# Spacing of the indirect row sends in the second half of a mixture-of-experts kernel

## The chip, the cores and the metric

The kernel runs on one core of one Trainium2 chip. The metric is the device time of one execution in microseconds (us). Engines are named as the profile names them: PE (matrix products), PEld (its weight loads), DVE (vector), ACT (scalar), POOL (GpSimd) and SP, which in this kernel only waits and issues DMAs.

## The reference, cut to what matters

```python
# x: (2, 512, 256), 1024 tokens of 256 values, f32
x = x + layernorm(attn(layernorm(x)))        # products, gates, a scan over time
x = x + layernorm(ffn(layernorm(x)))

def ffn(x):                                   # E = 64 experts, inner size 176, top 6 of 64
    probs = softmax(x @ gate_w.T)
    topk_w, topk_idx = top_k(probs, 6);  topk_w /= sum(topk_w)
    combine = sum(one_hot(topk_idx) * topk_w) # (tokens, 64)
    h = silu(einsum('th,eih->tei', x, experts_w1))
    y = einsum('tei,ehi->teh', h, experts_w2)
    routed = einsum('teh,te->th', y, combine)
    shared = (silu(g) * u) @ shared_down.T    # g, u = halves of x @ shared_gate_up.T
    return routed + shared
```

The kernel doesn't compute all experts for all tokens. It sends each token's row to a table, one stretch of 128 rows for an expert, and works through the experts one after the other.

## The kernel before, in words

The 1024 tokens are eight blocks `c` of 128. The first part of the kernel computes the attention-like layer and the gate. For each block it finds the six experts of each token (`choose`) and the row of the table `x_slots` in DRAM that the token's copy number `k` goes to (`place`, which writes `slot_i` and increments `slot_done`). A copy `(k, c)` is one indirect DMA from POOL, the function `send` (its record is line 567): 128 rows of 288 words (`W` = 256 + 32), 144 KB. There are 6 x 8 = 48 of them. The list `FIRST` holds 22, all for blocks 0 to 3, and `SECOND` holds 26, n = 0 to 25. Both lists use three semaphores in turn, by n modulo 3, each send adding 16 when it has landed. Before send n, POOL waits for the landing of send n - 3, so up to three are in flight. Some further waits hold certain sends until another engine's event: in `SECOND` one is at n = 6 (it needs the last slots), and at n = 13, 16 and 20 POOL waits for events of PE: `tx_ps` 1 (the first rows have been transposed), `h_ps` 1 (the first hidden product is done) and `tx_ps` 2. In `FIRST` there is one at n = 15 for `v_ps` 4.

The experts are taken in pairs t = 0 to 32 (64 experts and 2 spare stretches for overfull experts). SP loads the 128 rows of expert s into one of eight places of `early` (`load_rows`, line 392) and, from the seventh expert on, in every third turn a further pair's weights (`load_pair`, line 388). 16 pairs are loaded ahead. Before the rows of an expert, SP calls `rows_sent(e)` (line 403), which waits until enough sends of `SECOND` have landed. How many is fixed by hand in `sends_for`: the function returns 8 for expert 0, 10 for expert 1, 12 for expert 2, 16 for experts 3 to 5, 20 for 6 to 9, and all 26 from expert 10 on. SP works strictly in order: experts 0 to 7 in a first loop, then expert s + 8 after `token_done` for the pair of expert s.

On PE, pair t is `turn_rows(t)` (line 970, four transposes), `main(t)` (line 927), `rest(t)` (line 937) and `output(t)` (lines 949 and 953). For t = 2 to 5 PE runs, in this order, `turn_rows(t + 1)`, `main(t)`, `rest(t)`, `output(t - 1)`. So `main(t)` stands behind the transposes of the next pair. From t = 6 two pairs are taken together. DVE copies the transposed rows (line 1403), writes the token numbers (line 1410) and copies the outputs to `zbuf` (line 1419). ACT applies silu (lines 715, 716). After its sends, POOL scatters each expert's output to `y_rows` (line 609, 66 of them), in program order behind all the sends. At the end SP reads `y_rows` back, and PE and DVE add the six copies of each token with their weights, add the shared part and normalise.

Of the kernel before, what the change touches and what calls it, by code (L numbers as in the profile page):

```python
# [22 lines left out]
def moe_block(nc, x, w_act, w_rec, w_val, gate, pairs, w12, w2b, sgu, sd_a, sd_b, out):  # L23
# [28 lines left out]
    with ExitStack() as ctx:  # L52
# [3 lines left out]
        def sem(name):  # L56
            return ctx.enter_context(nc.semaphore(name))
# [167 lines left out]
        sent_second = [sem(f"sent_second{p}") for p in range(3)]  # L225
# [12 lines left out]
        tx_ps = sem("tx_ps")  # L238
        xT_done = sem("xT_done")
        h_ps = sem("h_ps")  # L240
# [250 lines left out]
        def _(pool):  # L491
# [73 lines left out]
            def send(k, c):  # L565

                return pool.indirect_dma_start(x_slots, bass.IndirectOffsetOnAxis(  # L567
                    ap=slot_i[:, c, k:k + 1], axis=0), rows[:, c, :], None)
# [1 line left out]
            pool.wait_ge(init_done, 16 * (E // 8 + 1))  # L570
            pool.wait_ge(slot_done, 1)
            for n, (k, c) in enumerate(FIRST):
                if n == 15:
                    pool.wait_ge(v_ps, 4)
                elif n == 19:
                    pool.wait_ge(x2T_ps, 4)
                elif n == 21:
                    pool.wait_ge(rank_ps, 2)
                if n >= 3:
                    pool.wait_ge(sent_first[n % 3], 16 * (n // 3))  # L580
                send(k, c).then_inc(sent_first[n % 3], 16)
            pool.wait_ge(slot_done, 2)
            for n, (k, c) in enumerate(SECOND):
                if n == 6:
                    pool.wait_ge(rank_ps, 3)
                    pool.wait_ge(slot_done, 3)
                elif n == 13:
                    pool.wait_ge(tx_ps, 1)
                elif n == 16:
                    pool.wait_ge(h_ps, 1)  # L590
                elif n == 20:
                    pool.wait_ge(tx_ps, 2)
                if n >= 3:
                    pool.wait_ge(sent_second[n % 3], 16 * (n // 3))
                send(k, c).then_inc(sent_second[n % 3], 16)
# [143 lines left out]
        def _(pe):  # L739
# [273 lines left out]
            def add_shared(c):  # L1013

                for j, (_, rows) in enumerate(SC):
                    w = sda_sb[:, j, :] if j < 2 else sdb_sb[:]
                    pe.matmul(in_sum(c), hidT[0:rows, j, P * c:P * c + P], w, start=(j == 0 and c % 2 == 0), stop=False)  # L1017
# [526 lines left out]
```

## Time and profile before

| | |
|---|---|
| median of 3 runs | 288.48 us (287.7 to 293.99) |
| profiled execution, device time | 288.84 us |
| its span (first to last recorded work) | 287.1 us |
| granted PE clock over the span | 0.929 |
| busy share of the span: PE, DVE, POOL, ACT | 82%, 61%, 45%, 28% |

The span is what the profile's times count from; 1.7 us of the execution's own time lies around it. Busy shares are means over stages with different limits: PE is busy for nearly all of the expert stage from 150 us on, but has gaps between 115 and 144 us. The profile's timeline gives, for each record or group of records, start, duration, engine, line, operation, and in brackets the idle time of the engine before it with what ended it.

### The profile page before, as it was taken

The page shows a single profiled execution, that of the slowest core. Times are in us where ns is not written, and L with a number is a line of the kernel's source. Part 1 is how long each engine was busy: PE and PEld are TensorE (multiplying, and loading weights), DVE is VectorE, ACT ScalarE, POOL GpSimd, SP SyncE. Part 2 cuts the span into 40 slices and gives each one's busy share as a digit, 9 for nine tenths or more (in the row PEclk, how much of TensorE's full clock was granted, in tenths as well). Part 3 has the DMA queues.
Part 4 walks back from the last instruction along what each step waited for, and adds up shares of the span by engine and source line. Part 5 has one row for each costly group of instructions (what it writes and reads, how often), then busy time and mean ns, then how long its engine had stood idle before and what let it go on. Part 6 is the DMA issues. An engine that isn't in the chain of part 4 may idle for free.

```text
span 287.1 us, 4229 instructions
## 1 busy us (share of the span) xinstructions
PE 236.2 (82%) x1382; PEld 178.7 (62%) x1382; DVE 176.4 (61%) x552; ACT 81.5 (28%) x188; POOL 129.2 (45%) x162
## 2 busy tenths in 40 slices
PE   6979939975488699065699999999999989989990
PEld 6534818552153568044377788888888767758880
DVE  4539896989997545462157788764443234544884
ACT  2586631394022114400011142112222402120033
POOL 7008300004677354757757606556556565561000
PEclk9999988999599689855979999999999999999997
DMA  6999999998232112345579999999969842668913
GB/s 211 356 376 370 371 360 416 423 415 331 87 123 103 62 62 84 126 142 168 194 203 308 350 371 348 309 384 348 308 238 364 281 153 75 219 222 277 345 39 110
DMA packets 34616, 72.00 MB, mean 251 GB/s; under 512 B 4577, under 2 KB 24609, under 8 KB 34081
## 3 DMA queue, kind: packets, MB, share of 16 engines
q1 hardware_dynamic: 29024, 55.68, 56.0%
q0 software_dynamic: 5568, 16.03, 14.9%
q8 instruction: 12, 0.20, 0.3%
q14 instruction: 12, 0.09, 0.1%
HBM read 44.89 MB, written 26.80 MB: 250 GB/s over the span
## 4 chain that ended last, share of the span: by engine, by line
PE 55%; DVE 20%; issue 9%; another core or an unknown queue 5%; DMA 4%; ACT 4%; POOL 1%; ACTq 0%; SPq 0%; POOLq 0%; DVEq 0%
PE bank L927 9%; PE bank L953 9%; PE bank L937 6%; PE bank L949 5%; PE bank L766 4%; PE bank L970 4%; PE bank L1017 4%; DMA early<-x_slots 3%; PE bank L775 3%; PE bank L802 3%; DVE stats L1082 2%; PE bank L836 2%; PE bank L1021 2%; DVE hidT L1131 2%
## 5 line engine op out<-in xcount | busy, mean ns | idle before, releaser
L609 POOL DMA_INDIRECT y_rows<-zbuf,token_i x66 | 64.9, 983 | 49.4 <-DVE zbuf L1419 33.8
L567 POOL DMA_INDIRECT x_slots<-rows,slot_i x48 | 47.4, 987 | 62.4 <-DVE slot_i L1234 34.5
L1419 DVE COPY zbuf<-bank 128x256 f32<-128x256 f32 x66 | 24.9, 420 | 56.1 <-PE bank L953 49.1
L715 ACT ACTIVATE sgu_sb<-bank 128x256 f32<-128x256 f32 x33 | 12.6, 383 | 108.1 <-PE bank L937 58.2
L927 PE MATMUL bank<-work,w_all 128*128 128x128 f32 x256 | 35.5, 290 | 5.6 <-issue 3.8
L927 PEld LDWEIGHTS bank<-work,w_all 128*128 128x128 f32 x256 | 33.1, 204 | 6.9 <-issue 6.7
L953 PE MATMUL bank<-w_all,sgu_sb 128*128 128x256 f32 x128 | 33.7, 397 | 0.0
L802 PE MATMUL bank<-x2nT,sgu_sb 128*128 128x256 f32 (+3 forms) x72 | 25.7, 511 | 7.4 <-DVE nt L1352 7.4
L970 PE MATMUL bank<-ident,early 128*128 128x128 f32 x128 | 20.0, 287 | 11.0 <-DMA early<-x_slots 11.0
L1403 DVE COPY work<-bank 128x512 f32<-128x512 f32 x33 | 22.5, 685 | 10.6 <-PE bank L970 5.4
L953 PEld LDWEIGHTS bank<-w_all,sgu_sb 128*128 128x128 f32 x128 | 22.5, 189 | 9.8 <-issue 7.6
L970 PEld LDWEIGHTS bank<-ident,early 128*128 128x128 f32 x128 | 15.5, 146 | 15.0 <-issue 6.9
L802 PEld LDWEIGHTS bank<-x2nT,sgu_sb 128*128 128x128 f32 (+1 forms) x72 | 14.4, 210 | 15.4 <-issue 13.6
L937 PE MATMUL bank<-work,w_all 128*64 128x128 f32 (+1 forms) x256 | 20.6, 294 | 0.8 <-issue 0.8
L949 PE MATMUL bank<-w_all,left 48*128 48x256 f32 x128 | 20.5, 421 | 0.7 <-ACT left L716 0.7
L937 PEld LDWEIGHTS bank<-work,w_all 128*64 128x64 f32 (+1 forms) x256 | 14.6, 136 | 3.8 <-issue 1.5
L766 PE MATMUL bank<-early,attw 128*128 128x512 f32 x32 | 14.5, 601 | 2.7 <-ACT early L680 2.0
L618 ACT ACTIVATE rs<-ve 128x2 f32<-128x2 f32 (+1 forms) x12 | 2.4, 204 | 46.5 <-DVE ve L1091 43.0
L775 PE MATMUL bank<-attw,early 128*128 128x256 f32 x64 | 14.1, 379 | 0.0
L949 PEld LDWEIGHTS bank<-w_all,left 48*128 48x128 f32 x128 | 10.7, 189 | 5.4 <-issue 3.7
L784 PE MATMUL bank<-wval_sb,zbuf 128*128 128x256 f32 x32 | 8.9, 440 | 5.6 <-issue 5.6
L775 PEld LDWEIGHTS bank<-attw,early 128*128 128x128 f32 x64 | 12.2, 190 | 2.1 <-issue 0.5
(218 smaller groups left out, 356.1 us busy)
## 6 DMA issues: line engine op xcount, KB each, us to landing
w_all<-pairs SPq DMA_DIRECT2D x32, 752.0 KB, 8.3
x_slots<-hidT SPq DMA_DIRECT2D x8, 1152.0 KB, 13.0
early<-x_slots SPq DMA_DIRECT2D x64, 144.0 KB
w_all<-y_rows SPq DMA_DIRECT2D x4, 1024.0 KB, 6.1
w_all<-y_rows SPq DMA_DIRECT2D x4, 512.0 KB, 10.4
y_rows<-zbuf,token_i POOLq DMA_INDIRECT x66
x_sb<-x SPq DMA_DIRECT2D x4, 256.0 KB, 3.6
out<-work SPq DMA_DIRECT2D x4, 256.0 KB, 2.1
```

The lines of the kernel that those rows point to most:

```text
L567: return pool.indirect_dma_start(x_slots, bass.IndirectOffsetOnAxis(ap=slot_i[:, c, k:k + 1], axis=0), rows[:, c, :], None)
L609: pool.indirect_dma_start(y_rows, bass.IndirectOffsetOnAxis(ap=token_i[:, s % 32:s % 32 + 1].bitcast(U32), axis=0), yS[:, s % 8, :], None) ...
L766: mm = pe.matmul(bank[4 + 2 * b + m][:], wact_sb[:, KC * late + k, m, :], xnT[:, k, b, late:late + T], start=(k == 0 and late == 0), stop= ...
L775: mm = pe.matmul(bank[c // 2][:, C * (c % 2):C * (c % 2) + C], xnT[:, k % KC, b, at:at + P], wrec_sb[:, k, :], start=(k == 0), stop=(k == ...
L802: mm = pe.matmul(product_in(n, g), sgu_sb[:, k, IS * g + at:IS * g + at + rows], x2nT[:, k, t0:t0 + width], start=(k == 0), stop=(k == KC ...
L927: pe.matmul(h_b[t % 2][:, P * i:P * i + P], w[:, PK * k + P * i:PK * k + P * i + P], xT[:, t % 4, i, k, :], start=(k == 0), stop=(k == KC ...
L937: mm = pe.matmul(h_b[t % 2][r:r + n, 2 * P:3 * P], w[:, at:at + n], xT[:, t % 4, i, k, :], start=(k == 0), stop=(k == KC - 1))
L949: pe.matmul(y_b[2 * (t % 2) + i][:, 0:C], hT_r[r:r + IR, t % 4, :], weights(2 * t)[r:r + IR, PW2 + 2 * C:PW], start=True, stop=False)
L953: mm = pe.matmul(y_b[2 * (t % 2) + i][:, 0:C], hT[:, t % 4, P * i:P * i + P], weights(2 * t)[:, PW2 + C * i:PW2 + C * i + C], start=False, ...
L970: mm = pe.transpose(x_b[t % 2][:, at:at + P], src[:, P * k:P * k + P], ident[:])
L1403: dve.tensor_copy(xT[:, t % 4].rearrange("p i k t -> p (i k t)"), x_b[t % 2][:]).then_inc(xT_done, 1)
L1419: dve.tensor_copy(yS[:, s % 8, :], y_b[s % 4][:, 0:C]).then_inc(y_done, 1)
```

## The change

Three waits for events of PE in `SECOND` (at n = 13, 16 and 20) are removed. In their place every send from n = 13 on first waits until the send ahead of it, n - 1, has landed. The wait for send n - 3 stays. In `FIRST` the wait for `v_ps` 4 stands one send earlier. What each send carries, their order, and the counts that SP waits for are as before.

```diff
             for n, (k, c) in enumerate(FIRST):
-                if n == 15:
+                if n == 14:
                     pool.wait_ge(v_ps, 4)
...
                 if n == 6:
                     pool.wait_ge(rank_ps, 3)
                     pool.wait_ge(slot_done, 3)
-                elif n == 13:
-                    pool.wait_ge(tx_ps, 1)
-                elif n == 16:
-                    pool.wait_ge(h_ps, 1)
-                elif n == 20:
-                    pool.wait_ge(tx_ps, 2)
+                if n >= 13:
+                    pool.wait_ge(sent_second[(n - 1) % 3], 16 * ((n - 1) // 3 + 1))
                 if n >= 3:
                     pool.wait_ge(sent_second[n % 3], 16 * (n // 3))
                 send(k, c).then_inc(sent_second[n % 3], 16)
```

## Rows read from the trace of the kernel before

**Rows 1.** The page: the span, the chain by engine, the scatters' group.

```profile
span 287.1 us, 4229 instructions
...
PE 55%; DVE 20%; issue 9%; another core or an unknown queue 5%; DMA 4%; ACT 4%; POOL 1%; ACTq 0%; SPq 0%; POOLq 0%; DVEq 0%
...
L609 POOL DMA_INDIRECT y_rows<-zbuf,token_i x66 | 64.9, 983 | 49.4 <-DVE zbuf L1419 33.8
```

**Rows 2.** Timeline of POOL: sends n = 9, 11, 12, 13, 15, 16, 19, 25.

```profile
118.20 0.96 POOL L567 DMA_INDIRECT x_slots<-rows,slot_i  x1 [0.30 <-issue]
...
120.73 0.96 POOL L567 DMA_INDIRECT x_slots<-rows,slot_i  x1 [0.30 <-issue]
121.99 0.96 POOL L567 DMA_INDIRECT x_slots<-rows,slot_i  x1 [0.30 <-DMA x_slots<-rows,slot_i]
124.09 0.96 POOL L567 DMA_INDIRECT x_slots<-rows,slot_i  x1 [1.15 <-PE bank L970]
...
126.67 0.96 POOL L567 DMA_INDIRECT x_slots<-rows,slot_i  x1 [0.30 <-DMA x_slots<-rows,slot_i]
128.88 0.96 POOL L567 DMA_INDIRECT x_slots<-rows,slot_i  x1 [1.25 <-PE bank L937]
...
132.67 0.96 POOL L567 DMA_INDIRECT x_slots<-rows,slot_i  x1 [0.30 <-issue]
...
140.51 0.96 POOL L567 DMA_INDIRECT x_slots<-rows,slot_i  x1 [0.30 <-issue]
```

**Rows 3.** Timeline of SP: row loads of experts 1, 2, 3, 6 and 10.

```profile
120.92 0.33 SPq L392 DMA_DIRECT2D early<-x_slots  x1
...
123.53 0.33 SPq L392 DMA_DIRECT2D early<-x_slots  x1
...
129.16 0.80 SPq L392 DMA_DIRECT2D early<-x_slots  x2
...
135.21 0.82 SPq L392 DMA_DIRECT2D early<-x_slots  x2
...
143.14 0.85 SPq L392 DMA_DIRECT2D early<-x_slots  x2
```

**Rows 4.** Timeline of PE: transposes of expert 3, and of pair 5.

```profile
131.27 0.69 PE L970 MATMUL bank<-ident,early 128*128 128x128 f32 x2 [2.87 <-DMA early<-x_slots]
...
150.74 0.60 PE L970 MATMUL bank<-ident,early 128*128 128x128 f32 x4
```

**Rows 5.** Timeline of DVE and ACT at the two events that POOL waited for.

```profile
123.85 0.69 DVE L1403 COPY work<-bank 128x512 f32<-128x512 f32 x1 [5.39 <-PE bank L970]
...
128.64 0.38 ACT L715 ACTIVATE sgu_sb<-bank 128x256 f32<-128x256 f32 x1 [10.56 <-PE bank L937]
```

**Rows 6.** DMA packets from 126.5 to 129.1 us, 40 slices of 0.065 us, busy tenths.

```profile
DMA  0000006999762000000000000099496920000000
```

**Rows 7.** Timeline of PE at pairs 2 and 3; then a window, PEclk third last.

```profile
143.89 2.05 PE L927 MATMUL bank<-work,w_all 128*128 128x128 f32 x8 [3.18 <-issue]
...
146.92 0.82 PE L970 MATMUL bank<-ident,early 128*128 128x128 f32 x4
147.57 1.06 PE L927 MATMUL bank<-work,w_all 128*128 128x128 f32 x8
...
149.14 0.70 PE L949 MATMUL bank<-w_all,left 48*128 48x256 f32 x4
...
143.00:150.00 7.00, 6.11 (x41) 4.96 (x42) 4.22 (x8) 0.98 (x4) 3.67 (x6) 0.76 0.68 200
```

**Rows 8.** Window 185 to 226 us: busy time (PE, PEld, DVE, ACT, POOL), PEclk, DMA share, GB/s.

```profile
185.00:226.00 41.00, 41.00 (x344) 35.35 (x343) 19.79 (x55) 11.13 (x43) 23.37 (x25) 1.00 0.93 324
```

**Rows 9.** Timeline of POOL: the last scatter.

```profile
258.13 0.96 POOL L609 DMA_INDIRECT y_rows<-zbuf,token_i  x1 [0.30 <-issue]
```

**Rows 10.** Timelines of PE and POOL at the moved wait of the first half.

```profile
81.95 3.72 PE L784 MATMUL bank<-wval_sb,zbuf 128*128 128x256 f32 x16 [0.77 <-issue]
...
86.64 0.96 POOL L567 DMA_INDIRECT x_slots<-rows,slot_i  x1 [0.30 <-DMA x_slots<-rows,slot_i]
```

## The prediction

> **What bounds the kernel now.** I read the page first, then the timeline of POOL over the sends of the second half, then that of SP for what the sends release, and last that of PE for when it needs what SP loads. The page's chain gives PE 55% of the span and POOL 1% [rows 1]. So POOL's 48 sends look free. They are not far from the path, though: SP may load the rows of expert 10 and of all later ones only when all 26 sends have landed, and in PE's program order everything from `main(4)` on stands behind the transposes of experts 10 and 11, that is `turn_rows(5)`. From there the expert stage is a train of PE work: from 185 to 226 us PE is busy 41.00 of 41.00 us, with DMA at 0.93 of its engines [rows 8]. A delay ahead of a train with no gap arrives at the end whole. The question is therefore how much later the last send lands, and how much slack stands between that and `turn_rows(5)`.
>
> **The slack.** Send 25 starts at 140.51 [rows 2]; SP issues the rows of expert 10 at 143.14 and those of expert 11 0.52 later, since the two issues together take 0.85 and one takes 0.33 [rows 3]. Expert 3's rows, issued at 129.16 [rows 3], were in PE's hands at 131.27 [rows 4], 2.11 us. So experts 10 and 11 are usable at 143.14 + 0.52 + 2.11 = 145.8, and PE comes to them at 150.74 [rows 4]. The slack is 5.0 us.
>
> **The spacing before.** Where nothing holds it, POOL starts a send 1.26 us after the last (120.73 to 121.99): 0.96 of its own work and 0.30 between two. From 121.99 (n = 12) to 140.51 (n = 25) there are 13 steps, 18.52 us [rows 2]. Of that 13 x 1.26 = 16.4 is bare pace and about 2.1 the held sends: 1.15 - 0.30 = 0.85 at n = 13 and 1.25 - 0.30 = 0.95 at n = 16 [rows 2], and about 0.3 in the rest. Removing the three waits gives back these 2.1 us at most.
>
> **The spacing after.** Each of the 13 steps becomes: start of a send, its landing, POOL waking, next start. No row shows a send waiting for the one right ahead, so I take it from two pieces. The first is start of a send to SP's issue that waited for it: n = 9 to expert 1, 118.20 to 120.92 = 2.72; n = 11 to expert 2, 2.80; n = 15 to expert 3, 2.49; n = 19 to expert 6, 2.54; n = 25 to expert 10, 2.63 [rows 2, 3]. The long ones are from an unbroken series of sends and the short ones from sends with a pause near them, as all will have after the change. I take 2.55. The second is POOL's wake: at `tx_ps` 1 DVE starts at 123.85 and POOL at 124.09, at `h_ps` 1 ACT at 128.64 and POOL at 128.88 [rows 2, 5], so POOL is 0.24 behind an engine woken by the same event. A step is 2.55 + 0.24 = 2.79, say 2.8. The packets bear it out: the burst of n = 15 (start 126.67) lies in slices 26 to 32 of the window, until about 128.6 [rows 6], 1.9 us after the start, before its completion can be seen.
>
> The bounds of a step: not under 1.9 + 0.24 = 2.14, since the packets end no earlier. From above 2.80 + 0.24 = 3.04 by the longest of the five, and with contention up to 3.8, since n = 12 started 3.79 after n = 9 without being held beyond the usual 0.30 [rows 2]. I take 2.8, nearest to the two short pairs.
>
> **The skill beside it.** The wait added here serialises the completion part of each transfer, and a rule speaks against that. By the Trainium skill, page "DMA: Bandwidth & Descriptors", section "Anatomy of one DMA — SWDGE (gpsimd) path", one DMA costs about 2.0 us plus its bytes over 436 GB/s, mostly the receipt of the write. For 147 KB this gives, as an estimate from that page, 2.34 us. If it counts from POOL's start the step would be 2.6 and the time about 300; if it comes on top of POOL's own 0.96 us the step would be 3.5, which is the second rival below. The 2.49 to 2.80 of the trace lie nearer to the first reading.
>
> **The sum.** Send 25 starts at 121.99 + 13 x 2.8 = 158.4 in place of 140.5. SP issues expert 10 at 158.4 + 2.55 = 160.9 (before: 143.14) and expert 11 at 161.5; PE gets them at 163.6. Against 150.74 that is 12.9 us late: 17.8 of delay, less the slack of 5.0.
>
> Earlier gates slip too, but behind this one. Send 15 lands at 121.99 + 3 x 2.8 + 2.55 = 132.9, so expert 3 is 3.8 late (129.16 before). Send 19 lands at 144.1 against 135.21, 8.9 late, and lets SP load experts 6 to 9; PE then reaches the end of pair 3 near 155 and stands idle for some 9 us. These slips cost nothing of their own.
>
> The idle PE has a price. After the gap at 143.89 pair 2 runs at the low clock: `main` and `rest` take 146.92 - 143.89 = 3.03 us, where those of pair 3 take 149.14 - 147.57 = 1.57, and the window 143 to 150 shows a granted clock of 0.76 [rows 7]. That 1.5 us is hidden in the new gap now, but `main(4)` and `rest(4)` pay the same after it: 1.5 us.
>
> Behind the waiting sends on POOL stand the scatters. They start 17.8 us later too, at about 159.7. The first scatters' buffers are wanted when pair 4 hands over its outputs, after 163.6 and several microseconds of products. A scatter takes 0.98 + 0.30 = 1.28 us [rows 1], two of them 2.6, while PE needs 3.3 us for a pair (41.00 us hold a bit over 12 pairs, judged by 344 / 28 products and transposes [rows 8]). So POOL catches up; its last scatter, at 258.13 before [rows 9], goes with the train. I add nothing. What SP holds back meanwhile are the loads of weights beyond the first 16 pairs. They are issued in step with the experts, many pairs ahead of use, and shift as a whole with PE. Nothing.
>
> The wait in the first half: `v_ps` 4 comes when the products of line 784 end, 81.95 + 3.72 = 85.67; send 14 of `FIRST` starts at 86.64, after the event [rows 10]. Nothing.
>
> Together 12.9 + 1.5 = 14.4 us. The profiled execution took 288.84 us (span 287.1 and 1.7 around it); it stands 0.4 above the median of 288.48. 288.84 + 14.4 = 303.2, which I give as 303.
>
> **The rivals.**
>
> *The slack swallows it (not slower).* The steps are so short that the last landing still falls inside the slack. Place: expert 11 at `turn_rows(5)`. It decides when the delay is under 5.0 us, so 13 steps under 18.52 + 5.0 = 23.5, a step under 1.81. Then the time is about 288.5; and if a landing were reported so early that POOL's own 1.26 ruled, the sends would end 2.1 us sooner and the time would be 287 to 288, since that too goes into slack. For it: the packets' burst is short, 0.5 us. Against it: packets still run 1.9 us after the start [rows 6]. 0.04.
>
> *Landings are slower than SP's issues let see.* The step is 3.5, between the 3.04 and the 3.8 that POOL's three-back waits allow [rows 2]. Then send 25 starts at 167.5, expert 11 is usable at 167.5 + 3.3 + 0.5 + 2.1 = 173.4, which is 22.7 late; with the clock's 1.5 the time is 313. Against it: n = 25 was seen landed by SP after 2.63. For it: row loads and sends would share the DMA. 0.12. (The second reading of the Trainium skill's page above is this case.)
>
> *A lone send lands faster.* With nothing else in flight the step is 2.2: send 25 at 150.6, expert 11 usable at 150.6 + 2.0 + 0.5 + 2.1 = 155.2, 4.5 late, with 1.5 the time is 295. For it: the shorter pairs are those with pauses. 0.12.
>
> **How the numbers follow.** The forecast (step 2.5 to 3.05) gets 0.72. At 2.5: 121.99 + 32.5 + 2.4 + 2.6 = 159.5, 8.8 late, with the clock 299; at 3.04: 121.99 + 39.5 + 2.8 + 2.6 = 166.9, 16.2 late, 306.5. I widen to 297 and 309 for half the clock's price, and for gaps later in the train that may take up or add a few us. That leaves 2 in 10 outside. A measurement of this kernel tells about 2% (5.8 us) from no change. Faster by more has 0.01, within 0.04, slower 0.95.
>
> **What would show it.** In the timeline of POOL, sends 13 to 25 start 2.8 us apart, and each idle time of about 1.8 us ends with the DMA of the sends. SP issues expert 10 at about 161. PE is idle for some 9 us before the transposes of pair 5 at about 163.6, and afterwards the distances between pairs are as before. Wrong would be: steps under 1.9 or over 3.1; a PE that doesn't wait at pair 5; or a train that runs closer together than before and wins the delay back.

## The result and the profile after

The changed kernel takes 303.14 us (median of 4 runs, 300.08 to 304.84), the kernel before 288.09 us in the same session. The ratio is 1.049, 95% interval 1.041 to 1.057. It compares the fast runs alone and comes to about 14 us, while the medians take in the slow runs too and differ by 15. The profiled execution of the changed kernel took 304.79 us with a span of 303.1, so it lies at the upper end of the runs; distances inside it are what is read here, not its total.

The page of the changed kernel, its span and its chain by engine, which answer to [rows 1]:

```profile
span 303.1 us, 4239 instructions
...
PE 54%; DVE 15%; issue 13%; POOL 6%; ACT 4%; another core or an unknown queue 3%; DMA 3%; ACTq 0%; SPq 0%; POOLq 0%; DVEq 0%
PE bank L949 9%; PE bank L923 9%; POOL x_slots L567 6%; PE bank L933 5%; PE bank L945 5%; PE bank L762 5%; PE bank L966 4%; PE bank L1013 4%; PE bank L780 3%; PE bank L798 3%; PE bank L771 3%; DVE stats L1078 3%; PE bank L1017 2%; PE bank L789 2%
```

POOL has gone from 1% of the chain to 6%, all of it the sends of line 567, and "issue" from 9% to 13%. Four source lines are gone, so PE's `turn_rows` is now line 966, `main` 923, `rest` 933, and `output` 945 and 949.

The timeline of POOL in the changed kernel: sends 12 to 15, 17, 21, and 25 with the first scatter. It answers to [rows 2].

```profile
120.63 0.96 POOL L567 DMA_INDIRECT x_slots<-rows,slot_i  x1 [0.30 <-DMA x_slots<-rows,slot_i]
123.32 1.07 POOL L567 DMA_INDIRECT x_slots<-rows,slot_i  x1 [1.74 <-DMA x_slots<-rows,slot_i]
126.19 0.96 POOL L567 DMA_INDIRECT x_slots<-rows,slot_i  x1 [1.79 <-DMA x_slots<-rows,slot_i]
128.88 0.96 POOL L567 DMA_INDIRECT x_slots<-rows,slot_i  x1 [1.74 <-DMA x_slots<-rows,slot_i]
...
135.22 0.96 POOL L567 DMA_INDIRECT x_slots<-rows,slot_i  x1 [2.64 <-DMA x_slots<-rows,slot_i]
...
146.92 0.96 POOL L567 DMA_INDIRECT x_slots<-rows,slot_i  x1 [2.56 <-DMA x_slots<-rows,slot_i]
...
157.80 0.96 POOL L567 DMA_INDIRECT x_slots<-rows,slot_i  x1 [1.75 <-DMA x_slots<-rows,slot_i]
159.07 0.96 POOL L605 DMA_INDIRECT y_rows<-zbuf,token_i  x1 [0.30 <-issue]
```

Each idle time before a send has become 1.73 to 1.80 us and ends with the landing of a send. Two are longer, 2.64 and 2.56: they are the first sends under way while SP loads rows (experts 3 to 5 and 6 to 9). From send 12 to send 25 there are now 37.17 us in place of 18.52.

SP's issue of expert 10's rows, and PE around its wait for them (answers to [rows 3, 4, 7]):

```profile
160.42 0.33 SPq L392 DMA_DIRECT2D early<-x_slots  x1
```

```profile
151.79 1.13 PE L949 MATMUL bank<-w_all,sgu_sb 128*128 128x256 f32 x4
162.74 0.66 PE L966 MATMUL bank<-ident,early 128*128 128x128 f32 x2 [9.81 <-DMA early<-x_slots]
163.89 0.69 PE L966 MATMUL bank<-ident,early 128*128 128x128 f32 x2 [0.49 <-DMA early<-x_slots]
164.37 1.92 PE L923 MATMUL bank<-work,w_all 128*128 128x128 f32 x8
...
171.14 1.81 PE L923 MATMUL bank<-work,w_all 128*128 128x128 f32 x8
```

PE stands idle for 9.81 us before the transposes of expert 10. Then `main(4)` to `main(5)`, 164.37 to 171.14, takes 6.77 us. The windows of the changed kernel show why, and that the later train is as it was in [rows 8] (columns: stretch, its length, busy PE, PEld, DVE, ACT, POOL, granted PE clock, DMA share, GB/s):

```profile
164.00:168.00 4.00, 4.00 (x22) 3.21 (x22) 2.04 (x4) 0.61 (x3) 3.11 (x5) 0.50 0.94 317
168.00:172.00 4.00, 4.00 (x17) 3.12 (x14) 1.37 (x4) 0.24 (x1) 2.02 (x3) 0.50 1.02 360
172.00:176.00 4.00, 4.00 (x29) 2.94 (x28) 1.63 (x7) 0.86 (x3) 1.51 (x2) 0.91 1.00 337
...
201.00:242.00 41.00, 41.00 (x343) 35.35 (x343) 19.81 (x55) 11.67 (x45) 23.34 (x25) 1.00 0.92 321
```

For 8 us after the gap the granted clock is the lower of the two levels (0.50, 1.2 GHz), and then it rises to 1.00 (2.4 GHz).

The front of the kernel, before send 12, differs between executions by more than some of the effects looked for: send 12 starts at 121.99 us in the profile of before and between 117.0 and 120.7 in all but one of the others. So I count times from the start of send 12. "Late" is against before.

| kernel | send 25, late | `main(4)`, late | `main` of pairs 24 and 25, late |
|---|---|---|---|
| before (from send 12: 18.52, 29.19, 97.97) | 0 | 0 | 0 |
| changed | 18.7 | 14.6 | 17.3 |
| landing waits from n = 18 | 14.1 | 10.0 | 11.3 |
| landing waits from n = 22 | 6.7 | 2.0 | 4.7 |
| two sends in flight (first, second time) | 1.0, 1.2 | -0.7, 2.2 | 0.2, 2.4 |
| no waits at all | -2.0 | 6.6 | 6.6 |

### The profile page after: what moved, and what is told of

The parts are those of the page before. It is cut to its first block, busy times and chain, and to the rows that moved or that the text cites. A ratio compares the mean times of both kernels' runs of the same rounds, so it can differ in the third digit from the quotient of the medians.

```text
span 303.1 us, 4239 instructions
## 1 busy us (share of the span) xinstructions
PE 241.6 (80%) x1382; PEld 181.2 (60%) x1382; DVE 175.2 (58%) x552; ACT 81.4 (27%) x188; POOL 128.7 (42%) x162
## 4 chain that ended last, share of the span: by engine, by line
PE 54%; DVE 15%; issue 13%; POOL 6%; ACT 4%; another core or an unknown queue 3%; DMA 3%; ACTq 0%; SPq 0%; POOLq 0%; DVEq 0%
PE bank L949 9%; PE bank L923 9%; POOL x_slots L567 6%; PE bank L933 5%; PE bank L945 5%; PE bank L762 5%; PE bank L966 4%; PE bank L1013 4%; PE bank L780 3%; PE bank L798 3%; PE bank L771 3%; DVE stats L1078 3%; PE bank L1017 2%; PE bank L789 2%
## 5 line engine op out<-in xcount | busy, mean ns | idle before, releaser
L605 POOL DMA_INDIRECT y_rows<-zbuf,token_i x66 | 64.2, 973 | 48.8 <-DVE zbuf L1415 34.2
L711 ACT ACTIVATE sgu_sb<-bank 128x256 f32<-128x256 f32 x33 | 12.7, 384 | 125.3 <-PE bank L933 54.3
L966 PE MATMUL bank<-ident,early 128*128 128x128 f32 x128 | 21.2, 299 | 27.8 <-DMA early<-x_slots 27.8
L923 PE MATMUL bank<-work,w_all 128*128 128x128 f32 x256 | 36.9, 299 | 2.9 <-DVE work L1399 1.8
L923 PEld LDWEIGHTS bank<-work,w_all 128*128 128x128 f32 x256 | 34.7, 214 | 4.2 <-issue 4.1
L949 PE MATMUL bank<-w_all,sgu_sb 128*128 128x256 f32 x128 | 34.6, 405 | 0.0
L798 PEld LDWEIGHTS bank<-x2nT,sgu_sb 128*128 128x128 f32 (+1 forms) x72 | 14.4, 209 | 15.9 <-issue 14.1
L762 PE MATMUL bank<-early,attw 128*128 128x512 f32 x32 | 16.2, 659 | 2.7 <-ACT early L676 2.0
L771 PE MATMUL bank<-attw,early 128*128 128x256 f32 x64 | 14.1, 379 | 0.0
L762 PEld LDWEIGHTS bank<-early,attw 128*128 128x128 f32 x32 | 6.4, 207 | 11.3 <-issue 7.9
```

Of the source, the lines that this page charges most:

```text
L605: pool.indirect_dma_start(y_rows, bass.IndirectOffsetOnAxis(ap=token_i[:, s % 32:s % 32 + 1].bitcast(U32), axis=0), yS[:, s % 8, :], None) ...
L762: mm = pe.matmul(bank[4 + 2 * b + m][:], wact_sb[:, KC * late + k, m, :], xnT[:, k, b, late:late + T], start=(k == 0 and late == 0), stop= ...
L771: mm = pe.matmul(bank[c // 2][:, C * (c % 2):C * (c % 2) + C], xnT[:, k % KC, b, at:at + P], wrec_sb[:, k, :], start=(k == 0), stop=(k == ...
L798: mm = pe.matmul(product_in(n, g), sgu_sb[:, k, IS * g + at:IS * g + at + rows], x2nT[:, k, t0:t0 + width], start=(k == 0), stop=(k == KC ...
L923: pe.matmul(h_b[t % 2][:, P * i:P * i + P], w[:, PK * k + P * i:PK * k + P * i + P], xT[:, t % 4, i, k, :], start=(k == 0), stop=(k == KC ...
L949: mm = pe.matmul(y_b[2 * (t % 2) + i][:, 0:C], hT[:, t % 4, P * i:P * i + P], weights(2 * t)[:, PW2 + C * i:PW2 + C * i + C], start=False, ...
```

## Experiment 1: the waits removed, nothing put in

```diff
-                elif n == 13:
-                    pool.wait_ge(tx_ps, 1)
-                elif n == 16:
-                    pool.wait_ge(h_ps, 1)
-                elif n == 20:
-                    pool.wait_ge(tx_ps, 2)
```

> The kernel before with its three waits for PE events (n = 13, 16, 20) taken out and nothing put in. My theory: these waits cost 2.1 us of POOL's time, the last send starts 2.1 us sooner, and the gain falls into the slack in front of pair 5, so the time stays within 1% of before, at most 1 us better. A rival, that the three waits protected something else (POOL's sends disturbing PE's first pairs) and their loss is part of the 15 us: 2 us or more slower than before.

Measured: 294.45 us, ratio to before 1.012 (1.002 to 1.022). The sends do end 2.0 us sooner, and the kernel is slower all the same, by about 3.5 us. The interval goes from 0.6 to 6.5 us, so the time alone rules out my gain but not a loss of under 1%; the trace, where everything from `main(4)` on is 6.6 us late, speaks for the rival. Its timeline, where the end of DVE's chain of small operations (`find_extra`), ACT's first silu and the second pair are read; PE's `rest(0)` ends at 126.4 in it ("remote" stands where the profile finds no releaser on this core):

```profile
128.41 0.96 POOL L567 DMA_INDIRECT x_slots<-rows,slot_i  x1 [0.30 <-issue]
128.82 0.23 DVE L1300 TENSOR_SCALAR ext_s<-ext_s,row_no 128x2 f32<-128x2 f32 x1 [0.36 <-DVE ext_s L1299]
...
130.94 0.96 POOL L567 DMA_INDIRECT x_slots<-rows,slot_i  x1 [0.31 <-issue]
130.95 0.15 DVE L1303 TENSOR_SCALAR ext_i<-rare_no 128x1 int32<-128x1 f32 x1 [1.26 <-issue]
132.21 0.96 POOL L567 DMA_INDIRECT x_slots<-rows,slot_i  x1 [0.30 <-issue]
132.35 0.15 DVE L1304 COPY nt<-ext_s 128x1 f32<-128x1 f32 x1 [1.25 <-DVE ext_i L1303]
...
137.25 0.96 POOL L567 DMA_INDIRECT x_slots<-rows,slot_i  x1 [0.30 <-issue]
138.67 0.38 ACT L709 ACTIVATE sgu_sb<-bank 128x256 f32<-128x256 f32 x1 [21.97 <-remote]
...
141.57 0.69 DVE L1397 COPY work<-bank 128x512 f32<-128x512 f32 x1 [9.06 <-remote]
...
142.41 2.04 PE L921 MATMUL bank<-work,w_all 128*128 128x128 f32 x8 [12.46 <-DVE work L1397]
```

The same two small DVE operations follow each other directly in before:

```profile
130.14 0.15 DVE L1309 TENSOR_SCALAR ext_i<-rare_no 128x1 int32<-128x1 f32 x1
130.33 0.15 DVE L1310 COPY nt<-ext_s 128x1 f32<-128x1 f32 x1
```

DVE waits there for its own last operation only. Where before they start 0.19 us apart, they now start 1.40 apart, each within 0.15 us after a start of a POOL send. ACT gets PE's first hidden product at 138.67, more than 12 us after it was done and 0.46 us after POOL's last send ends (137.25 + 0.96 = 138.21). The transposes of pair 1 end by 129.95, and DVE takes them at 141.57. All this lies in an unbroken series of 20 sends, 1.26 us apart. The waits of before cut this series into pieces of 7, 3, 4 and 6, with two scatters behind the last. In this execution no packet runs on the queues of instruction loads between 127 and 142 us, so instruction loads aren't what held ACT and DVE.

The kernel before has a smaller case of this itself, behind its last pause. PE ends the transposes of pair 2 at 138.58, and DVE takes them at 143.10, when POOL has started the last of eight DMAs in a row:

```profile
137.98 0.60 PE L970 MATMUL bank<-ident,early 128*128 128x128 f32 x4
...
143.10 0.69 DVE L1403 COPY work<-bank 128x512 f32<-128x512 f32 x1 [2.08 <-remote]
```

That bears on the slack that I read. With landing waits in the second half of the series (changed kernel, n = 18, n = 22) DVE takes pair 2 at once, and in the run from n = 22 PE is ready for the transposes of pair 5 at 25.7 us after send 12 in place of 28.8. A part of before's slack is time in which PE itself was held up.

## Experiments 2 and 3: fewer landing waits

```diff
                 elif n == 20:
                     pool.wait_ge(tx_ps, 2)
+                if n >= 22:      # in the other kernel: n >= 18
+                    pool.wait_ge(sent_second[(n - 1) % 3], 16 * ((n - 1) // 3 + 1))
```

> The kernel before, its three waits kept, with the wait for the send ahead only from n = 22 (4 sends). My theory: 4 x (2.75 - 1.26) = 6.0 us later for the last send, 5.0 of them slack before the transposes of pair 5, so about 1 us slower (0 to 2). Rival, that each wait costs its share at the end whole, with no slack (15 us over 13 waits): 4.6 us slower.

Measured: 292.12 us, ratio 1.011 (1.006 to 1.016), some 3.1 us slower, between the two expectations, so the total doesn't decide. The trace does: send 25 is 6.7 late (6.0 expected) and `main(4)` only 2.0, so 4.7 us were slack. But PE waited for expert 10's rows, and that had its own price:

```profile
149.88 1.30 PE L972 MATMUL bank<-ident,early 128*128 128x128 f32 x4 [4.42 <-DMA early<-x_slots]
...
150.98 1.92 PE L929 MATMUL bank<-work,w_all 128*128 128x128 f32 x8
...
157.75 1.65 PE L929 MATMUL bank<-work,w_all 128*128 128x128 f32 x8
```

```profile
150.00:157.00 7.00, 7.00 (x29) 4.97 (x30) 2.04 (x4) 0.85 (x3) 5.79 (x7) 0.50 0.93 279
```

`main(4)` to `main(5)` takes 6.77 us here too, and the granted clock is 0.50 from 150 to 157. A gap of 4.4 us cost as much clock as one of 9.8. At pair 24 this execution is 4.7 us late, which is the rival's figure; but it is made of 2.0 at `main(4)` and 3.2 of clock, less 0.5 made good on the way, and not of a share for each wait.

> The kernel before, its three waits kept, with the wait for the send ahead from n = 18 (8 sends). My theory: 8 x 1.49 = 11.9 us later, 0.8 more for one send that meets row loads, less 5.0 of slack = 7.7 us at pair 5, and 1.5 to 3 us at the low clock after the gap: 9 to 11 us slower than before. Rival, costs in proportion to the waits: 8 x 15 / 13 = 9.2 us; the two are told apart by the run from n = 22 and by the trace, where mine wants the PE gap before pair 5 to be about 4 us shorter than with all 13 waits.

Measured: 299.81 us, ratio 1.030 (1.020 to 1.040), 8.7 us slower by the ratio and 9.7 by the medians (9 to 11 expected). Send 25 is 14.1 late, `main(4)` 10.0. With the changed kernel these are three points: 6.7 to 2.0, 14.1 to 10.0 and 18.7 to 14.6, so the slack is 4.7, 4.2 and 4.1 us, and past it `main(4)` follows the last send nearly one to one. A cost in proportion to the number of waits, with no slack, would have put `main(4)` 6.7 late behind the first four waits.

The clock's part is not a fixed sum, though. Behind landing waits from n = 18 the gap before pair 5 is 12.1 us, and not about 4 shorter than in the changed kernel as I expected, since PE came to it sooner; and behind it `main(4)` to `main(5)` takes only 4.99 us. The granted clock is 0.50 at 160 to 162 us and back at 1.00 from 163 on, after 4 to 5 us of work:

```profile
158.14 0.66 PE L972 MATMUL bank<-ident,early 128*128 128x128 f32 x2 [12.09 <-DMA early<-x_slots]
...
159.78 1.92 PE L929 MATMUL bank<-work,w_all 128*128 128x128 f32 x8
...
164.77 1.06 PE L929 MATMUL bank<-work,w_all 128*128 128x128 f32 x8
```

So this restart cost 1.4 us where the other two cost 3.2.

## Experiments 4 and 5: the gate moved, and POOL's scatters held back

One number of the changed kernel: from which expert on SP asks for all 26 sends.

```diff
-        WITHOUT = (10, 6)
+        WITHOUT = (16, 6)
```

> The changed kernel with one number changed: SP waits for all 26 sends only from expert 16 on instead of expert 10 (experts 10 to 15 after 20 sends). POOL's sends and scatters stand exactly as in the changed kernel. My theory, that the late loads of experts 10 and 11 set the time: PE goes through pairs 5 to 7 without the 10 us gap, and then meets the next in line: rows of expert 16 (about 3.5 us late) and POOL's scatters, which start 17 us late and free the output buffers 4 to 6 us late. So 5 to 6 us slower than before, about 294 us, 8 us or more faster than the changed kernel. Rival, that the scatters queued behind the spaced sends are what costs: no gain, about 303 us.

Measured: 307.97 us, ratio 1.060 (1.049 to 1.071). My expectation of 294 missed by 14 us. Its first half held: pairs 4 and 5 ran with no gap (`main(5)` at 153.6 us). Then two things stood in line. First, `main(6)` stands behind the transposes of experts 16 to 19, whose rows SP may load only after the last send: PE's last wait before it is for the rows of expert 19. Second, ACT and DVE again got PE's work late, at the end of a series of POOL's DMAs. Beside these, DVE may write an output buffer only when the scatter of eight experts ago has landed, and the scatters start only behind the last send:

```profile
162.28 0.42 DVE L1415 COPY zbuf<-bank 128x256 f32<-128x256 f32 x1 [6.64 <-DMA y_rows<-zbuf,token_i]
...
169.09 0.69 PE L966 MATMUL bank<-ident,early 128*128 128x128 f32 x2 [2.87 <-DMA early<-x_slots]
169.57 3.39 PE L923 MATMUL bank<-work,w_all 128*128 128x128 f32 x16
...
177.06 0.96 POOL L605 DMA_INDIRECT y_rows<-zbuf,token_i  x1 [0.30 <-issue]
179.98 0.38 ACT L711 ACTIVATE sgu_sb<-bank 128x256 f32<-128x256 f32 x1 [23.89 <-remote]
180.19 0.69 DVE L1399 COPY work<-bank 128x512 f32<-128x512 f32 x1 [5.88 <-remote]
...
180.68 3.75 PE L923 MATMUL bank<-work,w_all 128*128 128x128 f32 x16 [5.67 <-ACT left L712]
```

Counted from send 12, pair 6 is 11.6 us late, pair 8 is 18.4 and pair 10 is 21.0. The 11.6 at pair 6 are the moved gate once more: the last send is itself 3.1 us later than in the changed kernel, with steps of 3.86 and 4.88 us beside the loads that now run early, and the rows of expert 19, issued at about 163, landed 6 us later beside weight loads. I had put the rows of expert 16 only 3.5 us late. The scatters held DVE, which took the rows of pair 7 at 164.79 for that reason, but that was over before expert 19's rows came; what the scatters alone cost this run doesn't show. From pair 6 to 8 the late events add another 7 us: PE waits 5.67 us for ACT. The run doesn't speak against the gate of the changed kernel, where PE's wait of 9.81 us ends with the rows; but it can't be taken as a clean proof of it either.

The next kernel adds waits to POOL, which can only delay it:

```diff
+                if s in (6, 8, 10):
+                    pool.wait_ge(scat[(s - 1) % 8], scattered(s - 1))
                 pool.wait_ge(y_done, s + 1)
```

> The kernel that asks for all 26 sends from expert 16 on, with three added waits on POOL: scatters s = 6, 8 and 10 wait for the landing of the scatter ahead. This only delays POOL, by about 5 us. Theory A (an unbroken series of POOL's DMAs holds back the events of the other engines): ACT gets the hidden product of pair 6 at once and not 6 us after its end, and the kernel is faster than without the waits, 300 to 304 against 308 us. Theory B (the scatters are simply late): 2 to 5 us slower than 308.

Measured: 313.42 us, ratio 1.088 (1.080 to 1.095): slower, as theory B said, and by more than its 2 to 5 us (5.4 by the medians; by the ratios, taken to the kernel before as it ran beside each, it is more). But the place that theory A spoke of did change. ACT takes pair 6 as soon as `rest` gives it, and pairs 6 and 8 stand 5.2 us apart in place of 11.1:

```profile
170.97 3.36 PE L925 MATMUL bank<-work,w_all 128*128 128x128 f32 x16
174.26 1.09 PE L935 MATMUL bank<-work,w_all 128*64 128x128 f32 x16
...
176.21 1.95 PE L925 MATMUL bank<-work,w_all 128*128 128x128 f32 x16
```

```profile
174.97 0.38 ACT L713 ACTIVATE sgu_sb<-bank 128x256 f32<-128x256 f32 x1 [17.86 <-PE bank L935]
```

At pair 8 this kernel is 12.7 us late where the one without the pauses is 18.4. It loses more later, since the three added waits last 4.18, 6.57 and 4.56 us where I had counted about 5 for all three: with the DMA engines busy a landing takes far longer. So each theory got one part: the pauses cleared the events, and their length cost more than that.

## Experiments 6 to 8: the price of the clock

> The changed kernel once more, as the base for the run with the filled gap on the same chip: 300 to 305 us, PE idle about 10 us before the transposes of pair 5, then about 8 us at the low clock.

Measured: 302.98 us, ratio 1.037 (1.025 to 1.048) with a before of 292.85 us in that session. That is 10 to 11 us in place of 14 to 15: the changed kernel took the same time as in the first session, and the kernel before took 4.8 us more. The intervals of the two ratios overlap. `main(4)` to `main(5)` is 6.8 us again.

```diff
             for t in range(2, QUADS[0]):
+                if t == 4:
+                    pe.wait_ge(y_done, 6)
+                    keep_warm(y_b[0], 18)     # in the second kernel: 10
                 turn_rows(t + 1)
```

> The changed kernel, with 18 spare products of 128x512 (about 8 us) on PE into a free bank between pair 3's output and the transposes of pair 5, where PE stands idle. Nothing else waits for them. Theory: of the 15 us, 3.2 are pairs 4 and 5 at the low clock after the gap (6.77 us from one main to the next where before took 3.60). With the gap filled the distance is 3.6 again and the time about 3 us below the changed kernel. Rival, that the distance is long because these two pairs wait for late rows or semaphores: no gain, or a loss.

Measured: 304.04 us, no gain. The 18 products took 15.7 us, not 8: I had taken each record for a whole product, and a product of this kind leaves two. They outlasted the gap, and `main(4)` came at 165.5, counted from send 12 about 3.7 us later than in the changed kernel. But the distance that the theory is about is 3.6 us in place of 6.8 (`main(4)` 165.47, `main(5)` 169.07), with a granted clock of 1.00:

```profile
166.00:170.00 4.00, 4.00 (x33) 3.16 (x31) 2.63 (x7) 0.85 (x3) 1.77 (x3) 1.00 0.99 325
```

So the same two pairs take 3.2 us less when PE doesn't come out of an idle stretch. And though `main(4)` starts 3.7 us later than in the changed kernel, pair 24 (233.9) is only 0.5 later, both from send 12. What the overrun cost was won back by the higher clock, and the total is where it was.

> The changed kernel with 10 spare products in PE's gap (0.87 us each at the high clock, 8.7 us) in place of 18, which took 15.7 us and outlasted the gap. The clock theory: pairs 4 and 5 run at the high clock, main to main 3.6 us in place of 6.8, and the end comes 3 us sooner than in the changed kernel, about 300 against 303.

Measured: 304.39 us, no gain as far as the figures of different sessions can be compared (ratio 1.059, 1.049 to 1.070, to a before of 288.26), and the distance is 6.2 us. The ten products end at 157.3, and PE is idle for 2.1 and 0.6 us before pair 5's rows. The clock fell all the same, after this short gap and well into the work:

```profile
157.00:160.00 3.00, 0.65 (x3) 0.20 (x2) 0.00 (x0) 0.00 (x0) 2.39 (x3) 1.00 0.72 215
160.00:164.00 4.00, 3.61 (x22) 2.58 (x22) 2.11 (x4) 0.85 (x3) 3.17 (x5) 0.66 0.93 280
164.00:168.00 4.00, 4.00 (x16) 3.36 (x15) 1.61 (x5) 0.00 (x1) 2.86 (x3) 0.50 1.03 363
```

So the price of the clock is shown at its place, by the run with 18 products: 3.2 us where the gap was filled against where it wasn't, and 1.4 behind the gap of the run from n = 18. That a well-sized filler would lower the total is not shown.

## Experiments 9 to 12: where pauses are enough

Three landing waits in the places of the three event waits:

```diff
+                if n in (13, 16, 20):
+                    pool.wait_ge(sent_second[(n - 1) % 3], 16 * ((n - 1) // 3 + 1))
```

> The kernel before with its three waits for PE events replaced by a wait for the send ahead at the same three places (n = 13, 16, 20) only. The run without these waits was 3 us slower though its sends ended sooner: ACT and DVE got PE's events 11 us late, while POOL issued 20 sends without a pause. Theory A, that any pause in POOL's series lets these events through: no late first pair, the last send 2 to 3 us later than before inside the slack, time as before within 1%. Theory B, that it is the event waits themselves that matter (the order they force between PE and POOL): about 3 us slower than before, like the run with no waits.

Measured: 294.75 us against 292.85, ratio 1.008 (0.998 to 1.018). Between the theories, and inconclusive as a total. In its trace the first pairs are on time (`main(1)` at 134.40, `main(2)` at 142.77), so event waits aren't needed for them. The late events come afterwards, in the series behind the last pause: 6 sends, 4 scatters and 2 fills of spare rows from 137.41 on, and ACT and DVE receive PE's work 15.09 and 10.70 us after their last own (153.19 and 154.66).

The changed kernel with two sends in flight:

```diff
-                    pool.wait_ge(sent_second[(n - 1) % 3], 16 * ((n - 1) // 3 + 1))
+                    pool.wait_ge(sent_second[(n - 2) % 3], 16 * ((n - 2) // 3 + 1))
```

> The changed kernel with each send from n = 13 waiting for the one two ahead, so two are in flight. Theory of spacing: a step is (2.50 + 0.24) / 2 = 1.37 us in place of 2.75, the last send lands within the slack, and the time is that of before. With theory A beside it (POOL's series must have pauses): POOL waits only 0.1 to 0.4 us between sends, and whether such short waits are enough is open; if not, the first pair's events come late as without any wait, 3 us or more slower.

Measured: 288.65 us against 292.85, ratio 0.987 (0.976 to 0.997). Two sends take 2.72 us where nothing else is in the way, 1.36 a step, and the last send is 1.0 us late, inside the slack: against the changed kernel of the same session (302.98 us) the whole loss is gone. The count of sends in flight, one against two, is what the cost hangs on. Whether POOL's short waits, here up to 1.1 us over the usual 0.30, are enough to let the events through was left open, and the answer is: not quite. ACT gets the first hidden product 4.0 us after `rest(0)` ends (before: 0.9; in the trace of the repeated run below 2.2), and `main(1)` starts 14.1 us after send 12 in place of 10.8 (repeated: 11.7). PE has made this good by `main(4)` in the first trace and not in the second. Since the ratio suggested a gain, it ran again with more rounds:

> The kernel with two sends in flight from n = 13 once more, with more rounds. If its 1.3% over before is real, the ratio is again 0.98 to 0.995; if it was the scatter of the runs, the interval holds 1.

Measured: 287.12 us against 288.26, ratio 0.996 (0.992 to 1.000). The gain isn't confirmed; the kernel is as fast as before, or up to 0.8% faster.

> Two sends in flight from n = 13, and two scatters of the output stage (s = 47 and 50) wait for the landing of the scatter ahead, 1.8 us each. In all traces PE, ACT and DVE meet events that come late at pair 28, during POOL's series of 8 scatters. Theory A (pauses in POOL's series let the others' events through): pair 28 to 29 takes 3.6 us in place of 5.6 to 5.9, total 2 us better than with two in flight. Theory B (what is late there has another cause): no change, or up to 2 us worse from the later scatters.

Here two scatters wait for the landing of the one ahead:

```diff
+                if s in (47, 50):
+                    pool.wait_ge(scat[(s - 1) % 8], scattered(s - 1))
```

Measured: 287.80 us against 288.26, ratio 0.998 (0.994 to 1.002), no gain over two in flight. At its own place theory A held: from pair 27 to 29 it takes 7.2 us in place of 9.2 to 9.5 in the traces of before and of two in flight. But in this trace a stretch of late events came up at the end, at pair 31 (`main(31)` 243.76, `main(32)` 250.69, 6.9 us in place of 3.2). The traced execution was the longest of the twelve (291.47 us), so it doesn't tell whether the others had this stretch; why the total didn't gain stays open. No version was found that beats the kernel before beyond doubt.

## Why the prediction was right, point by point

- **The gate.** Right. SP's issue of expert 10 follows send 25 by 2.62 us (157.80 to 160.42; 2.55 predicted), PE's wait before pair 5 ends with that load, and three numbers of landing waits gave a line with a slack, then one to one.
- **The step.** Predicted 2.8, measured 2.69 to 2.87 in eleven of thirteen and 3.61 and 3.51 where row loads ran beside; mean 37.17 / 13 = 2.86. The two pieces, landing and wake, were right, and the contention was left out. The delay of the last send was 18.7 us, predicted 17.8.
- **The figure of the Trainium skill** (page "DMA: Bandwidth & Descriptors", section "Anatomy of one DMA — SWDGE (gpsimd) path"). The second reading (a step of 3.5) is refuted by the 2.69 us. The first, about 2.6, lies 0.1 below the quiet steps.
- **The slack.** Predicted 5.0, measured 4.1. The term that was off is the load of the rows: 2.11 us for one in [rows 4], but expert 11's rows, issued at 160.80 with four other loads right behind, were there at 163.89, 3.1 us later.
- **The clock.** The direction was right, the size wrong: 1.5 us predicted, 3.2 measured. The 1.5 was read from pair 2 in [rows 7], where the clock fell only as pair 2 began (1.00 from 138 to 143 us, 0.50 from 144 to 147) and was back after some 3 us. In the changed kernel it had fallen at about 156, inside the gap, and stayed low until almost 173, over 9 us of work. That the stretch behind the new gap would be as short as that of pair 2 was taken over without a reason. Nor is 3.2 a fixed price: the run from n = 18 lost 1.4.
- **The train.** Right: the lateness is 17.7 us at pair 5, 17.3 at pair 24 and 17.4 at the end of the span. A delay ahead of it isn't made good.
- **The scatters.** No cost, as predicted, but for a weaker reason than given. They were hidden by the gate, which was later still. With the gate moved (experiment 4) they held DVE, but up to pair 8 what PE waited for last was something else.
- **The wait in the first half.** Wrong in detail. Send 14 of the first half was held, as the changed kernel's timeline of POOL shows:

```profile
86.70 0.95 POOL L567 DMA_INDIRECT x_slots<-rows,slot_i  x1 [1.07 <-PE bank L780]
```

  1.07 us idle in place of 0.30; it is 0.77 us, and disappears in the 4.46 us that POOL waits for PE before the last send of that half.
- **The three waits removed.** The prediction gave their removal up to 2.1 us of gain and nothing else. That was incomplete: alone, it costs 3.5 us (experiment 1). In the changed kernel the landing waits make pauses of their own, so this cost is not in the 15 us.
- **The sum.** The total came out better than its terms. Against the profile of before, the terms as measured make 18.65 - 4.10 + 3.17 = 17.7 us, not 14.4; the span grew by 16.0, as this execution reached send 12 by 1.36 us sooner and the train gave back 0.4. The median of all runs lies 1.7 below this profiled execution. So 303 matched the median of 303.14 partly by luck: a front that varies by a few us from one execution to the next stood against terms that were 3.3 us too small together. In the second session the same change cost 10 to 11 us (experiment 6).

## What to carry to other kernels

A transfer that waits for the one ahead costs its full time to landing in place of the time to issue it (2.75 against 1.26 us here); with two in flight nearly all of that is hidden. Whether it matters is read where the last of them is waited for: measure the slack there, and count a restart at the low clock (1.4 to 3.2 us here) behind any gap it opens in a busy PE. A wait that looks like mere delay may be what keeps the other engines fed, so take it out alone before trusting that it is free.

## What the runs showed of the hardware that I had not expected

- **Late events in an unbroken series of POOL's indirect DMAs.** With sends 1.26 us apart and no pause, small DVE operations that wait for each other start 1.40 us apart and not 0.19, in step with POOL's issues, and PE's results reached ACT and DVE up to 12 us late, until the series ended. It showed with the waits gone and behind the last pause of three, and it vanished at the place where pauses were put in (11.1 to 5.2 us between two pairs). Short pauses (two sends in flight) left 2 to 4 us of it at the first pair. That the series causes it is so supported by runs on both sides; by what path it acts stays open. That instruction loads are not the path in experiment 1 rests on the absence of their packets in that stretch.
- **A landing under load.** The landing of a 144 KB send took 2.5 us on quiet DMA engines, and a POOL wait for the landing of a scatter lasted 4.2 to 6.6 us where these engines were busy.
- **The clock after a gap.** A gap of 4.4 us brought the same 9 us of work at 1.2 GHz as one of 9.8, and one of 12.1 us only 4 to 5; with gaps of 2.1 and 0.6 us behind 8.9 us of steady work the clock fell as well. The length of the gap doesn't tell the price in these runs.
